# Row maxima over all 128 rows of TensorE with zeroed halves, work placed in half steps, and PSUM buffers given out by a small table of times

## What is computed

```python
q = (x @ Wq).reshape(N, S, HEADS, HEAD_DIM).transpose(0, 2, 1, 3)
k = (x @ Wk).reshape(N, S, HEADS, HEAD_DIM).transpose(0, 2, 1, 3)
v = (x @ Wv).reshape(N, S, HEADS, HEAD_DIM).transpose(0, 2, 1, 3)
logits = jnp.einsum('nhid,nhjd->nhij', q, k) * scale
causal = 1000000000.0 * (jnp.tril(jnp.ones((S, S), dtype=logits.dtype)) - 1.0)
logits = logits + causal[None, None, :, :]
attn = jax.nn.softmax(logits, axis=-1)
out = jnp.einsum('nhij,nhjd->nhid', attn, v)
...
x = _layernorm(x + _L0_attn_ref(...), axis=-1)
x = _layernorm(x + _L0_ffn_ref(...), axis=-1)
x = _layernorm(x + _L1_attn_ref(...), axis=-1)
x = _layernorm(x + _L1_ffn_ref(...), axis=-1)
```

## Time and profile before

| | us |
|---|---|
| median of 3 runs | 994.16 (993.75 to 994.36) |
| the profiled execution's own time | 990.67 |
| its span in the trace | 988.8 |
| first attention in it: from start to the last unit | about 752 |
| unit 3 begins on PE | 41.15 |
| step 43 begins on PE (jobs of the third pair) | 159.33 |
| steps 83, 123, 163, 203, 243, 283 begin | 247.66 to 689.28, each 88.3 after the one before |

### The profile page before, as it was taken

The page is one execution under the profiler, slowest core; times in us unless marked ns, Lnnn a source line. Parts: engine busy times, 40 slices in busy tenths (PEclk is TensorE's granted clock), DMA queues, the critical chain, the costliest instruction groups (busy, mean ns, idle before and its releaser), DMA issues. The chain is left out here.

```text
span 988.8 us, 25900 instructions
## 1 busy us (share of the span) xinstructions
PE 794.8 (80%) x10965; PEld 540.7 (55%) x10965; DVE 593.2 (60%) x1026; ACT 688.1 (70%) x953; POOL 623.7 (63%) x393
## 2 busy tenths in 40 slices
PE   5777888999899899989989998999996667343390
PEld 2344554666566566656655665666665555233390
DVE  5675666667566566656665665566676576565015
ACT  4356676888788788878878887888995675331262
POOL 6255765978787788978797887879003564313350
PEclk9699999999999999999999999999997997665595
DMA  5211132130131013012202301130004400030262
GB/s 158 51 34 28 23 82 61 33 82 2 34 66 33 18 35 82 2 34 55 44 3 50 81 2 34 34 65 3 3 2 133 139 1 2 0 86 21 57 197 87
DMA packets 58060, 48.31 MB, mean 49 GB/s; under 512 B 6602, under 2 KB 54344, under 8 KB 57814
## 3 DMA queue, kind: packets, MB, share of 16 engines
q1 hardware_dynamic: 56198, 43.60, 18.4%
q0 software_dynamic: 1024, 1.45, 0.5%
q10 hardware_dynamic: 720, 1.57, 0.4%
HBM read 16.64 MB, written 5.26 MB: 22 GB/s over the span
## 5 line engine op out<-in xcount | busy, mean ns | idle before, releaser
L636 POOL TENSOR_TENSOR prob_lo<-prob,prob_hi 128x896 f16<-128x896 f32 (+2 forms) x286 | 517.7, 1833 | 155.5 <-ACT prob L464 150.9
L520 DVE TENSOR_REDUCE part_max<-psum 128x2 f32<-128x1024 f32 (+1 forms) x320 | 334.9, 1063 | 153.9 <-PE psum L327 94.0
L461 ACT ACTIVATE prob_hi<-psum 128x1024 f16<-128x1024 f32 (+1 forms) x320 | 297.6, 931 | 146.5 <-PE psum L375 142.8
L464 ACT ACTIVATE prob<-psum 128x1024 f32<-128x1024 f32 (+1 forms) x320 | 297.8, 933 | 0.0
L372 PE MATMUL psum<-high 128*128 128x512 f16 (+3 forms) x640 | 226.5, 354 | 35.3 <-DVE kq L502 14.2
L395 PE MATMUL psum<-v,prob_hi 128*128 128x65 f16 x2176 | 231.6, 193 | 3.7 <-DVE prob_lo L561 3.0
L399 PE MATMUL psum<-v,prob_lo 128*128 128x65 f16 x2176 | 230.9, 194 | 0.0
L397 PE MATMUL psum<-v,prob_hi 128*128 128x64 f16 x2176 | 230.2, 192 | 0.0
L375 PE MATMUL psum<-mixed 65*128 65x512 f16 (+3 forms) x640 | 221.5, 351 | 0.0
L395 PEld LDWEIGHTS psum<-v,prob_hi 128*128 128x128 f16 x2176 | 201.3, 98 | 35.0 <-DVE prob_lo L561 10.3
L397 PEld LDWEIGHTS psum<-v,prob_hi 128*128 128x128 f16 x2176 | 200.4, 97 | 25.7 <-issue 0.6
(11 more groups left out here) (226 smaller groups left out, 1081.4 us busy)
## 6 DMA issues: line engine op xcount, KB each, us to landing
high<-kq SPq DMA_DIRECT2D x128, 128.0 KB
mixed<-kq SPq DMA_DIRECT2D x64, 128.0 KB
ew<-in_L_ffn_W SPq DMA_DIRECT2D x32, 256.0 KB, 5.0
expert_rows<-heads_out SPq DMA_DIRECT2D x1, 1032.0 KB, 7.1
e_xe<-expert_rows SPq DMA_DIRECT2D x4, 258.0 KB, 3.8
prob<-in_L_attn_x SPq DMA_DIRECT2D x4, 256.0 KB, 6.4
mixed<-shift SPq DMA_DIRECT2D x64, 1.0 KB
eb<-in_L_ffn_b SPq DMA_DIRECT2D x1, 1024.0 KB
```

The lines of the kernel that those rows point to most:

```text
L461: act.activation(m.prob_hi[i % HI_RING][:, 0:u.width], src, ACT.Exp, scale=EXP_SCALE)
L464: act.activation(m.prob[i % PROB_RING][:, 0:u.width], src, ACT.Exp, scale=EXP_SCALE)\
L520: last = dve.tensor_reduce(m.part_max[:, g % 2, :, r, c:c + 1], src[:, :, col:col + width], AX, ALU.max)
L636: pool.tensor_tensor(m.prob_lo[i % LOW_RING][:, c], m.prob[i % PROB_RING][:, c], m.prob_hi[i % HI_RING][:, c], ALU.subtract).then_inc(low_ ...
```

## The change

1. A max job's matmuls take all 128 rows. The stationary operand holds one head's queries and zeros in the other head's rows, and the moving operand holds both heads' keys. For that `kq` grows from four planes to five: rest of the queries, queries of the even head over zeros, keys, queries of the odd head under zeros, rest of the keys. The zeros are written once, at the start, by DVE and POOL. The mask is added by one 128-row matmul a block and side, where four of 64 rows and their four DMAs for the operand `half` were.
2. The high parts of a kq job no longer lie side by side for both heads. ACT writes them with three instructions in place of one (128 partitions x 512, then twice 64 x 512), and DVE's rest is three in place of one.
3. For odd heads the copies of `kq` by DMA are four in place of three.
4. The plan has half steps. At step i PE does the jobs of half step 2i, S(i+2), the jobs of 2i+1, W(i-1). ACT and DVE follow in the same order: after exponentials i ACT does the copies of half steps 2i-3 and 2i-2, and DVE those of 2i before the riding shift and those of 2i+1 after it.
5. The jobs of the first pair are spread up to half step 28, and those of the second begin there and not at step 17. In a pair's list of jobs kq 0 and kq 1 now come together at its beginning, and kq 2 and 3 four jobs ahead of the last blocks that need them, not two.
6. `place_all` plays the whole order through with a small table of times (nanoseconds for filling and draining each kind) and gives each thing the buffer that is free first.

```diff
@@ pair_jobs
-    return (kq[0:1] + top[0][:-1] + kq[1:2] + top[0][-1:] + top[1][:-2] + kq[2:3] + top[1][-2:] + top[2][:-2]
-            + kq[3:4] + top[2][-2:] + v + top[3])
+    return (kq[0:2] + top[0] + top[1][:-4] + kq[2:3] + top[1][-4:] + top[2][:-4]
+            + kq[3:4] + top[2][-4:] + v + top[3])
+
+
+def spread_jobs(plan, jobs, begin, end):
+
+    at = [begin + k * (end - begin) // len(jobs) for k in range(len(jobs))]
+    for h, job in zip(at, jobs):
+        plan[h].append(job)
+    return at
...
@@ place_all
+    def place(what, fill, reader, drain):
+        nonlocal riders
+        b = min(range(BUFS), key=lambda b: (max(free[b], clock["pe"]), free[b]))
+        what.buf, what.turns = b, made[b]
...
+        clock["pe"] = max(clock["pe"], free[b]) + fill
+        clock[reader] = max(clock[reader], clock["pe"] + 500) + drain
+        free[b] = clock[reader]
...
+            if job.kind == "max":
+                width = sum(width for _, _, _, width in job.blocks)
+                place(job, 2 * width + 50, "dve", 5 * width + 200)
...
+            elif job.kind in ("kq", "v"):
+                place(job, 3072, "act", 2400)
+                free[job.buf] = clock["dve"] = max(clock["dve"], clock["act"]) + 2800
...
@@ PE, maxima
-                        rows = slice(side * HD, (side + 1) * HD)
                         o = out[:, side * 512 + col:side * 512 + col + width]
-                        last = pe.matmul(o, m.kq_hi[rows, 1, q], m.kq_hi[rows, 0, k], start=(n == 0), stop=(c < g),
+                        last = pe.matmul(o, m.kq[:, 1 + 2 * side, q], m.kq[:, 2, k], start=(n == 0), stop=(c < g),
                                          skip_group_check=True)
-                    if c == g:
-
-                        for h in range(2):
-                            for side in range(2):
-                                end = side * 512 + col + width
-                                rows = slice(side * HD, (side + 1) * HD)
-                                last = pe.matmul(out[:, end - P:end], m.half[rows, h, 0, :], m.half[rows, h, 1, :],
-                                                 start=False, stop=(h == 1), skip_group_check=True)
+                        if c == g:
+                            last = pe.matmul(o[:, width - P:width], m.identb, m.mask_ik, start=False, stop=True,
+                                             skip_group_check=True)
@@ PE, the loop over units
             for i in range(NU):
-                for job in PLAN[i]:
+                for job in PLAN[2 * i]:
                     run(job)
                 if i + 2 < NU:
                     scores(UNITS[i + 2])
+                for job in PLAN[2 * i + 1]:
+                    run(job)
                 if i > 0:
                     weigh(UNITS[i - 1])
@@ ACT, kq_high
-                act.activation(m.kq_hi[:, :, c], m.buf[job.buf].rearrange("p (b n) -> p b n", b=2), ACT.Copy)\
-                    .then_inc(high_done, 1)
+                act.activation(m.kq[:, 2, c], m.buf[job.buf][:, 0:512], ACT.Copy)
+                act.activation(m.kq[0:HD, 1, c], m.buf[job.buf][0:HD, 512:1024], ACT.Copy)
+                act.activation(m.kq[HD:P, 3, c], m.buf[job.buf][HD:P, 512:1024], ACT.Copy).then_inc(high_done, 1)
@@ DVE, kq_low
-                dve.tensor_tensor(m.kq_lo[:, :, c], m.buf[job.buf].rearrange("p (b n) -> p b n", b=2), m.kq_hi[:, :, c],
-                                  ALU.subtract).then_inc(free[job.buf], 1)
+                dve.tensor_tensor(m.kq[:, 4, c], m.buf[job.buf][:, 0:512], m.kq[:, 2, c], ALU.subtract)
+                dve.tensor_tensor(m.kq[0:HD, 0, c], m.buf[job.buf][0:HD, 512:1024], m.kq[0:HD, 1, c], ALU.subtract)
+                dve.tensor_tensor(m.kq[HD:P, 0, c], m.buf[job.buf][HD:P, 512:1024], m.kq[HD:P, 3, c], ALU.subtract)\
+                    .then_inc(free[job.buf], 1)
```

More of the change, by code:

```diff
@@ L169, in place_all @@
-    halved = [what for what in order if isinstance(what, Job) and what.kind in ("kq", "v")]
-    for n, job in enumerate(halved):
-        job.place = n
-    return {(job.pair, job.group): job for job in halved if job.kind == "kq"}
-KQ = place_all()
+    free, made = [0] * BUFS, [0] * BUFS
+    holder = [None] * BUFS
+    clock = {"pe": 0, "act": 0, "dve": 0}
+    riders = halved = 0
+    keys = {}
+    def place(what, fill, reader, drain):
+        nonlocal riders
+        b = min(range(BUFS), key=lambda b: (max(free[b], clock["pe"]), free[b]))
+        what.buf, what.turns = b, made[b]
+        what.after = holder[b].rider if isinstance(holder[b], Unit) else None
+        made[b] += 1
+        holder[b] = what
+        clock["pe"] = max(clock["pe"], free[b]) + fill
+        clock[reader] = max(clock[reader], clock["pe"] + 500) + drain
+        free[b] = clock[reader]
+        if isinstance(what, Unit) and what.rider is not None:
+            what.rider.ride, what.rider.buf = riders, b
+            riders += 1
@@ new lines, in run @@
+    def run(jobs):
+        nonlocal halved
+        for job in jobs:
+            if job.kind == "max":
+                width = sum(width for _, _, _, width in job.blocks)
+                place(job, 2 * width + 50, "dve", 5 * width + 200)
+            elif job.kind == "shift":
+                place(job, 200, "dve", 500)
+            elif job.kind in ("kq", "v"):
+                place(job, 3072, "act", 2400)
+                free[job.buf] = clock["dve"] = max(clock["dve"], clock["act"]) + 2800
+                job.place = halved
+                halved += 1
+                keys[job.kind, job.pair, job.group] = job
@@ L178 @@
+    run(PLAN[-1])
+    for i in range(-2, NU):
+        if i >= 0:
+            run(PLAN[2 * i])
+        if i + 2 < NU:
+            place(UNITS[i + 2], 2 * UNITS[i + 2].width, "act", 4 * UNITS[i + 2].width + 400)
+        if i >= 0:
+            run(PLAN[2 * i + 1])
+        if i > 0:
+            clock["pe"] += UNITS[i - 1].width * 5 // 3
+    return tuple({(pair, group): job for (kind, pair, group), job in keys.items() if kind == name} for name in ("kq", "v"))
+KQ, VALUES = place_all()
 class Memory:
@@ L261, in spread_count @@
     def spread_count(head):
-        return (head // 3 + 1) * CHUNK
+        return 16 * sum(4 + h % 2 for h in range(head % 3, head + 1, 3))
     with nc.Block() as block:
@@ L384, in weigh @@
                 wait_low(pe, u.index)
+                if u.first and u.group % 2 == 0:
+                    job = VALUES[u.head // 2, u.group // 2]
+                    pe.wait_ge(free[job.buf], job.turns + 1)
                 if u.first and u.turn > 1:
```

113 lines of the change are left out of this document (49 added, 64 removed).

## The result

The change makes the kernel slower. The median goes from 994.03 us (993.75 to 994.36, 4 runs) to 1010.81 us (1009.49 to 1012.68, 4 runs), a ratio of 1.017 with a 95% interval of 1.0152 to 1.0188. The forecast was 989.1, and the range ended at 1000.

A forecast was written before the change was run, and what follows sets the result against it. In six like pairs, PE's work and how long kq or v jobs hold one of three buffers set the time. Start +1.9, up to step 43 -6.0, pairs -1: 990.67 to 985.6 us profiled, median 989.1; range 978 to 1000.

The forecast's parts named there:

- Matmuls: PE's max jobs: 128 rows cost 0.43 us for 0.42, +0.9 in all, plus 6 for lost shared switches.
- The 6 us for shared switches: Before step 43, 29 of 288 max jobs follow another and share its switches; each loses 0.2 us with 128 rows.
- the estimate of 1045: Far end of rival 3: by the full 2x for 64-row matmuls, 58 us of columns come on top, some 1045.
- Copies: Three instructions on ACT and DVE: kq_high 1.58 us for 1.02, kq_low 1.88 for 1.20, buffer held about 1.25 longer.
- Half steps, a pair: Pairs from the third on: -2.4 at kq 0 and 1, +1.05, +1.35, -0.4, +0.1: -0.3 us; six pairs about -1.
- The walk: Stalls traced at four places a pair: kq 0 and 1 1.3 us, kq 2 1.95, kq 3 2.3, v 0.6.
- Up to step 43: From unit 3 to step 43: 91.6 of work, 3.5 added, 17.1 of stalls make 112.2 us for 118.2, -6.0.
- The dense circle: Up to step 43, max job, scores and reduction on alternating buffers: tightest circle 2.74 us instead of 3.07.
- The start: Up to unit 3: the 1.7 us DMA wait goes, longer first copies and more jobs come; 43.0 for 41.15, +1.9.
- Rival 1: Slower: the longer hold is not covered at a pair's start, S(87) waits for kq 1; up to 14 us, 1002, chance 0.17.
- Rivals 3 and 4: Rival 3: max matmuls side by side worth more, 1000, chance 0.04; 4: gain up to step 43 only 3, 992, 0.17.
- rival 2: Much faster: the hold is hidden, by cheap copies or kq 2 and 3 stalls staying at 0.9; 970 us, chance 0.14.

The follow-up runs named there:

- rows_only: The kernel before with 128-row max matmuls, five planes, three copies and three rests, in the old order and buffer turns: 1064.48 us, ratio 1.0725.
- copies_three: The kernel before with only each kq job's copy and rest split into three instructions, matmuls still 64 rows: 1067.6 us, ratio 1.0775.
- busy: The changed kernel with six more 512-column matmuls, results overwritten, in one max job a pair ahead of the wait for kq 3: 1007.26 us, ratio 1.0153.
- order_copies: The kernel before with the new order (points 4 to 6) and both copies and rests in three, 64-row matmuls kept: 1017.01 us, ratio 1.0243.
- act_three: The kernel before with the new order (points 4 to 6) and only ACT's copy in three, 64-row matmuls kept: 991.81 us, ratio 0.9997.

## Why the prediction was wrong

By its own steps, from 985.6 forecast for the profiled execution to 1010.98 measured, 25.4 us:

1. *Matmuls.* Right for a job by itself: 0.46 was forecast and measured, and PE's work in a pair is 81.8 before and 81.9 after. The 6 us for shared switches before step 43 no run isolates: rows_only was to pay them and came 3 us below copies_three, with 71.7 us at 1.2 GHz for 95.6. The Trainium skill, TensorEngine Tiling (Array Packing), Theoretical Speedup, gives up to 2x for a small dimension of 64 or less, and the estimate of 1045 goes by the full 2x; here a lone job of two such matmuls comes to none of it, 0.42 for the 0.43 of two in turn. That a change of tiling mode drains the engine (the Trainium skill, TensorEngine Tiling (Array Packing), Key Properties) agrees with the 0.1 us on either side of such a job in the earlier trace rows.
2. *Copies.* The direction was right, the term too small: 1.67 and 1.98 for 1.58 and 1.88. The earlier trace rows had it. Two instructions of 512 take 1.10 with 0.49 between the starts, so the last one takes 0.61; I let the third add the distance of the starts, 0.49, where it adds a whole 0.6. On DVE likewise 0.69 for 0.6. The hold grew by 1.43 and not by 1.25.
3. *Half steps, a pair.* This is the step that failed: -0.3 forecast, +1.6 measured at full clock, +17.6 for -1 over six pairs. The walk had each stall at the right place and each too small: S(86) by 0.37 (0.2 from the copies and rests, 0.07 from the rider's copy, 0.1 between the end of that and S(86)), kq 3 by 0.2, from the longer hold, and kq 2 by 0.4. And it left out one, a max job's buffer behind v of 0.78, where I counted only v itself: 0.6 for 1.50. These make 1.9 a pair, 11 us. Besides, six times -0.3 is -1.8, which the sum took as -1.
4. *The clock.* It stood nowhere in the sum. The granted clock of 1.00 from 60 us to the end of the attention was taken over from before without a reason, where before has no stall longer than 1.5 us there: five of six pairs dip behind the stall of 2.5, at 1.62 each, 8 us; busy shows cause and price. Steps 3 and 4 together are the 19.4 us between -1.8 and +17.6.
5. *Up to step 43.* -1.35 for -6.0. Of the 4.65, 1.4 are stalls, 18.5 for 17.1 (kq 1 of the first pair alone waits 3.0). The other 3.2 stays open: the dip of 6.8 us at 83.6 may cost up to 3.4, but before has 6.6 us at 1.2 GHz in this stretch too, up to 48 us, which the 91.6 of work already held. The dense circle was forecast at 2.74, and steps 30 to 35 are 2.70 apart, where they were 3.2. Step 43 began at 161.1 and not near 154.
6. *The start.* +3.15 for +1.9. Unit 3 begins at 41.41 with the order alone (+0.3), at 42.71 with split copies alone (+1.6), at 45.93 with both (+4.8, order_copies). What makes both together more than their sum I did not follow; these are single executions, and two of the same program differ by 1.0 here (44.30 and 43.32). *After step 283*: 0.0, as forecast.

Rival 1 named the right sign and cause, a longer hold that is not covered, at 0.17. It was put at a pair's start, with a price of 14 us, and the prediction told the reader to look at S(87). S(87) does not wait; the loss is behind kq 2, kq 3 and v. Rivals 3 and 4 were wrong, rival 2 was far off.

The sum hid a larger fact. It set the order's gain against the copies' price as two small numbers, -0.3 a pair. On the chip, in the new order, they are -26 us for the order, +50 for the copies and rests (0.9738 to 1.0243), and -7 for the matmuls. An error of some tenths on either side of a difference of two such terms decides its sign.

## What to carry to other kernels

Where an engine already waited for a buffer, each 0.1 us of longer hold cost 0.1 us at that wait, whichever engine added it and though ACT and DVE had 17 and 34 us a pair free; count the instructions between filling and release before all else, at the duration of a whole further instruction and not at the distance of the first two starts. Read for each stall not only its sum but its longest single wait, since the clock can fall behind it. And cost a change of several parts part by part against the kernel without the others: here the best kernels have the order (points 4 to 6) and nothing else of the change.

## What the runs showed of the hardware

- Two 64-row max matmuls side by side, with the switches there and back, take as long as two 128-row ones in turn, 0.42 and 0.43 us, and the kernels in the old order 1067.6 and 1064.5. Yet in the new order, with nearly equal stalls (7.6 and 8.1 a pair), the trace of the 64-row kernel had 58.0 us at 1.2 GHz and that of the 128-row kernel 23.9.
- The granted clock fell for 3.4 us, at a price of 1.62, behind a single stall of 2.5 us in an engine that is 92% busy over the pair; 1.3 us of added work ahead of the stall made it stay up. It did not fall behind the stalls of 1.67 and 1.81 in the same kernel, nor behind that of 2.5 in one pair of six, but did behind 1.76 in act_three, so the length of the stall alone does not say it.
- A copy from PSUM of 64 partitions by 512 takes as long as one of 128 partitions by 512, 0.58 to 0.60 us on ACT and 0.67 to 0.69 on DVE, in either order.
